# A two-layer decoder in one program: the first shared-head key rows ahead of the gates in the last stage

## What is computed

```python
def _L1_ffn_ref(x, W_gate, W_qkv):            # H = 16 heads of hd = 32
    gating = softmax(x @ W_gate.T, axis=-1)
    idx = argmax(gating, axis=-1)
    indicator = one_hot(idx, H)
    gating_top1 = indicator * max(gating, axis=-1, keepdims=True)
    q, k, v = split(x @ W_qkv.T, 3, axis=-1)
    k_shared = einsum('bth,bthd->btd', indicator, k)
    v_shared = einsum('bth,bthd->btd', gating_top1, v)
    att = softmax(causal(einsum('bhqd,bkd->bhqk', q, k_shared) / sqrt(hd)))
    return einsum('bhqk,bkd->bhqd', att, v_shared)
x = _layernorm(x + _L1_attn_ref(x, ...))      # "P" in the kernel: x3 -> x4
x = _layernorm(x + _L1_xattn_ref(x, ctx, ...))  # "C": x4 -> x5
x = _layernorm(x + _L1_ffn_ref(x, ...))       # "H" and "A": x5 -> x6
```

## Time and profile before

| | us |
|---|---|
| median of 3 runs | 2414.94 (2409.84 to 2415.85) |
| profiled execution | 2439.16 |
| its span, first to last instruction | 2437.4 |
| TensorE matmul busy (PE) | 2190.3 (90% of the span) |
| VectorE busy | 1196.0 (49%) |
| ScalarE busy | 499.0 (20%) |
| GpSimd busy | 437.7 (18%) |
| mean granted TensorE clock | 0.95 |

### The profile page before, as it was taken

The page is one execution under the profiler, slowest core; times in us unless marked ns, Lnnn a source line. Parts: engine busy times, 40 slices in busy tenths (PEclk is TensorE's granted clock), DMA queues, the critical chain, the costliest instruction groups (busy, mean ns, idle before and its releaser), DMA issues. The chain is left out here.

```text
span 2437.4 us, 30877 instructions
## 1 busy us (share of the span) xinstructions
PE 2190.3 (90%) x12423; PEld 1263.0 (52%) x12431; DVE 1196.0 (49%) x1787; ACT 499.0 (20%) x751; POOL 437.7 (18%) x445
## 2 busy tenths in 40 slices
PE   5888889877999989789999957999999999999996
PEld 3434444323444466455555534566666666666554
DVE  2456666645777752002222225445665665646455
ACT  1443444440000021111111101211222222222111
POOL 1111111112444402201111031000111111100001
PEclk9999999987999999899999978999999999999998
DMA  7000000004111046331211150010010101000000
GB/s 252 1 1 27 27 27 18 27 9 168 30 30 33 27 152 192 76 125 61 63 63 61 57 203 15 13 44 27 18 35 18 35 18 35 2 27 10 1 10 18
DMA packets 63857, 125.26 MB, mean 51 GB/s; under 512 B 12878, under 2 KB 13973, under 8 KB 63733
## 3 DMA queue, kind: packets, MB, share of 16 engines
q1 hardware_dynamic: 37492, 61.56, 7.6%
q10 hardware_dynamic: 19536, 43.26, 5.7%
q0 software_dynamic: 6704, 18.64, 2.6%
HBM read 92.18 MB, written 39.70 MB: 54 GB/s over the span
## 5 line engine op out<-in xcount | busy, mean ns | idle before, releaser
L863 PE MATMUL convB_conv<-kv,toep 128*128 128x512 f32 x640 | 277.8, 597 | 9.9 <-POOL kv L849 9.9
L863 PEld LDWEIGHTS convB_conv<-kv,toep 128*128 128x128 f32 x640 | 122.6, 192 | 165.1 <-issue 156.6
L2045 DVE RECIPROCAL tail_inv<-tail_ring 128x256 f32<-128x256 f32 x64 | 112.4, 1756 | 188.5 <-PE tail_ring L1575 188.5
L1294 PE MATMUL moe_gu_ps<-gu,moe_xT 128*128 x624 | 193.7, 464 | 2.2 <-DVE moe_xT L1357 2.2
L1294 PEld LDWEIGHTS moe_gu_ps<-gu,moe_xT 128*128 128x128 f32 x624 | 119.5, 192 | 79.9 <-issue 22.9
L849 POOL TENSOR_TENSOR kv<-vT,cT 128x512 f32 (+1 forms) x128 | 132.8, 1068 | 147.3 <-PE convB_conv L863 133.4
L888 DVE TENSOR_REDUCE vT<-prod 128x512 f32 (+1 forms) x128 | 138.1, 1079 | 16.7
L1823 POOL TENSOR_SCALAR_AFFINE_SELECT tail_expT<-tail_expT 128x1024 f32<-128x1024 f32 x64 | 71.0, 1109 | 350.8 <-ACT tail_expT L1894 350.5
L1312 PE MATMUL moe_y_ps<-down,moe_hT 128*128 (+1 forms) x234 | 110.7, 609 | 12.5 <-ACT moe_hT L1346 12.5
L1817 POOL TENSOR_TENSOR tail_rstd_x<-tail_rstd_x,const_minus_half 128x2 f32<-128x2 f32 x32 | 22.5, 704 | 516.6 <-DVE tail_rstd_x L1997 516.6
L503 POOL TENSOR_SCALAR_AFFINE_SELECT front_expT<-front_expT 128x2048 f32<-128x2048 f32 x32 | 64.1, 2004 | 277.5 <-ACT front_expT L558 277.5
(11 more groups left out here) (318 smaller groups left out, 3810.9 us busy)
## 6 DMA issues: line engine op xcount, KB each, us to landing
y_slots<-moe_y ACTq DMA_DIRECT2D x39, 256.0 KB
toeplitz<-filt_pad SPq DMA_DIRECT2D x1, 8192.0 KB, 32.8
toep<-toeplitz SPq DMA_DIRECT2D x32, 256.0 KB, 2.6
gu<-in_L_ffn_gate_up_proj ACTq DMA_DIRECT2D x2, 2816.0 KB
gu<-in_L_ffn_gate_up_proj SPq DMA_DIRECT2D x2, 2816.0 KB
front_e<-in_ctx SPq DMA_DIRECT2D x8, 512.0 KB, 4.7
x_after<-x SPq DMA_DIRECT2D x8, 512.0 KB, 5.1
down<-in_L_ffn_down_proj ACTq DMA_DIRECT2D x2, 2048.0 KB
```

Source lines behind the costliest of these rows:

```text
L863: ins = pe.matmul(conv[:, NC * p + lc, :], toep[p][:, lo:lo + P], kv[p][:, c].rearrange("p b i j -> p (b i j)"), start=c == 0, stop=c == lc)
L1294: ins = pe.matmul(gu_ps[:, s % 2, h, 0:HID], xT[:, c, :], wgu[c][:, e, h * HID:(h + 1) * HID], start=c == 0, stop=c == NC - 1)
L2045: link.after(dve.reciprocal(inv[c % 2][:], bank[:, S:2 * S]))
```

## The change

In the loop over rounds TensorE does the first key rows ahead of the gates; before, the gates came first.

```diff
                     if H_: turn("H", "x5", h)
                     if A_: shared_out(a)
-                    if H_: turned("H", h); gates(h); rows("H", "k", h, 0, xT[h % 2], wide["gk"])
+                    if H_: turned("H", h); rows("H", "k", h, 0, xT[h % 2], wide["gk"]); gates(h)
                     if P_: shift("P", p)
```

## The result

| | before | after |
|---|---|---|
| median of six runs, us | 2415.39 | 2403.57 |
| ratio of after to before | | 0.9951 (95%: 0.9938 to 0.9965) |
| profiled execution, us | 2439.16 | 2402.52 |
| its span, us | 2437.4 | 2400.6 |

The kernel became 0.49% faster, 11.8 us. The same kernel was timed twice more beside the one before: ratio 0.9957 (0.9943 to 0.9970; 2405.02 against 2414.75) and, on another chip on which the kernel before takes 2437.8 us, 0.9959 (0.9945 to 0.9972; 2429.07). So 9 to 12 us are won; 7.1 were forecast. One of the six runs of after took 4532.67 us, for a reason that the record does not show; the ratio leaves it out, and without it the median is 2403.09.

The account below looks back on a forecast made before the run. TensorE's own time was taken to bound the last stage. Four clock falls of 1.70 us (6.8) plus 0.3 us from weight loads gave 7.1 us less, from 2414.94 to 2407.8 us; range 2402.5 to 2413.5.

Parts of the forecast that it names:

- What bounds the kernel: Last stage: TensorE's own time is the time, so what is saved there reaches the end.
- The cause of the long rounds: Rounds 2 to 7: 4.65 us of short matmuls and gaps halve TensorE's clock, costing 1.70 us in four rounds.
- the rival by which short matmuls are not the cause: Gaps ahead of the gates, left unchanged, lower the clock; nothing happens, time 2414.9 us; chance 0.06.
- Wait in front: Before the first key rows: they wait for the same two semaphores as the gates did; cost nothing.
- seam: Key rows to shift: exposed and hidden first weight loads change places; -0.05 us a round, -0.3 over six.
- what gets later: Gates' result comes 3.5 us later for VectorE and ScalarE; hidden, with 2.1 us to spare at the shift's copy.
- The lead of 2.88 us: Transposes and gaps ahead of the first key rows: no clock fall was expected in this stretch.
- The sum: Whole kernel: 6.8 us from the clock plus 0.3 from weight loads, 7.1 us less; median 2407.8.
- The loop's terms: Rounds 2 to 7: four clock falls of 1.70 us removed, and 0.05 us a round from weight loads.
- the full success: At most one clock fall left in rounds 2 to 7, gain 5 to 11 us; chance 0.72.
- The rival of falls that stay in part: Rounds 2 to 7: one to two of four clock falls remain or move; gain 0 to 4 us; chance 0.16.
- the forecast's case: At most one clock fall left in rounds 2 to 7; gain 5 to 11 us, 2403 to 2410; chance 0.72.

## Why the prediction came out as it did

**What bounds the kernel.** Right. What TensorE saves in the rounds reaches the end: four rounds are 1.7 us shorter each.

**The cause of the long rounds.** Right, and now shown from both sides: useless wide work ahead of the gates takes the falls away (0.9971), and more narrow work brings falls back (1.0051). The rival by which short matmuls are not the cause falls with these two.

**Wait in front, seam, what gets later.** Right to a few tenths. The keys start with the same wait of 0.35 us. The seam gives 0.10 us a round (5.46 to 5.36) where I took 0.05. The gate copy was put at about 1992.1 on the clock of the old round, 5.5 us behind the step's start, and comes 5.47 us behind it (1962.04 less 1956.57). The pick of the values was to start 0.2 us late and does. The copy of the shift was to end 2.1 us ahead of its use and ends 2.2 ahead.

**The lead of 2.88 us.** Right. No fall starts in it in the three profiles of after; since profiles repeat one another in the loop, that is six different rounds rather than 18. The Trainium skill, in "TensorE: Matmul & The Clock Gate", Part 4, holds that transposes do not count as PE-busy the way matmuls do; by that alone some falls should have stayed. None did behind this lead of 2.87 us with its 16 transposes, and no run here parts transposes from gaps.

**The sum.** Its sign was right and it was too small: 7.1 us against 11.8, 9.7 and 8.7 in three comparisons, and 10.2 in the profiles. The loop's terms hold: 4 x 1.70 and 6 x 0.08 to 0.10 make 7.3, and 0.3 more come at the loop's end, where the transposes at L1485 take 1.32 us instead of 1.63. What is missing is a term for the written-out end. Over its last 84 us the granted clock is 0.81 in before and 0.85 in after: 2.7 to 3.1 us, less 0.3 to 0.5 ahead of it. I had read the end as unchanged because its instructions are. The step that failed is "No work is added or taken away" taken to mean that the unchanged rest costs what it did; the runs with shifted work show that it does not: with 0.86 us added far ahead, the last stretch takes 83.84 us and no longer 80.9 to 81.3. The 1.6 us between the 10.2 of the profiles and the 11.8 of the first comparison are within the scatter of the runs.

**How sure.** The sentence that each execution has its own number of falls was wrong: two unlike rounds of one execution did not show it. The second profile of before has the same four, and so the spread of 6.0 us among the runs does not come from them in any way shown here. The profiles point ahead of the stage: two of after differ by 6.7 us in their span (2407.4 and 2400.6), and 6.4 of these lie before the first keys of round 2 (1622.13 and 1615.71). Which instructions make it stays open. I put the full success on the edge of 0.3% with 0.47 for faster and 0.50 for no difference; with the count of falls fixed and the end included it would have lain clear of the edge. The range of 2402.5 to 2413.5 holds the time, near its lower end, and that is luck in part: the lower end allowed for executions with more than four falls, of which none was seen, and the time lies there because of the written-out end. The rival of falls that stay in part was also added up wrongly: with one or two falls left, 7.1 less 1.7 or 3.4 is a gain of 3.7 to 5.4 us, not 0 to 4, and one fall left is counted in the forecast's case as well.

## What to carry to other kernels

Look for places where a bounding TensorE has transposes, short waits and narrow matmuls in a row. Here 4.65 us of them cost 1.70 us in the wide work behind, in four rounds of six, and 2.87 us cost nothing. Wide work put in between kept the short stretches from joining; that is worth a trial as long as the engine that reads the narrow result has that much idle time. Before and after such a move, count the stretches at half clock over the whole stage, not only where code was moved: a shift of a microsecond can take one away or bring one back far behind. And the narrow result can be delayed only as far as its reader's own order allows: in the loop 3.5 us were free, of the next 3.65 us 1.4 were paid by TensorE, and behind the loop a wait of 2.14 us came with the first 3.5.

## What was not expected of the hardware

Useless work made the kernel faster: 0.86 us a round of added matmul, 6.4 us less in all. The falls of the clock repeat from one execution to the next with the same program, in the same rounds and with the same lengths of rounds to 0.02 us (115.39 and 115.40), though the two executions reach the stage 26 us apart. Behind the loop they do not always repeat: two profiles of the changed kernel have the clock at 1.00 and at 0.79 over the same place, and yet need the same time to the end within 0.4 us. And 0.86 us of added work in the midst of busy work cost 3.0 us.
